# An attention and feed-forward kernel: stationary operands of 4, 32, 33 and 64 rows or columns widened to 128, and four small transposes made one

## The chip, the cores and the metric

The kernel runs on one core of a Trainium2 chip. The metric is the device time of one launch in microseconds; the kernel before takes 800.02 us (median of three runs, 799.88 to 800.47).

## What is computed

The input x has 8 batches of 512 tokens with 128 channels, float32. Three blocks follow each other, each with a residual:

```
x = x + 0.5 * ffn(layernorm(x))
x = x + attention(layernorm(x))
x = x + 0.5 * ffn(layernorm(x))
```

The feed-forward block has 512 hidden units, an exact GELU, and weights that depend on the batch: products of even and odd rows of tokens 1 to 16, scaled by 0.001, are added to both weight matrices.

```
even, odd = lt[:, ::2, :], lt[:, 1::2, :]          # lt: tokens 1 to 16 of x
m1 = (even[:, :4, :, None] * odd[:, :4, None, :]).reshape(B, 512, 128)
h = gelu(x @ W1.T + scale * x @ m1.T + b1)
out = h @ W2.T + scale * h @ m2.T + b2
```

The attention has 16 heads of 64. Queries and keys are RMS-normalised. The score of query i and key j gets a causal bias that depends on a learned gate of the key:

```
gate = softplus(einsum('bthd,hd->bht', k, u_n) / sqrt(64))
bias = -max(i - j, 0) * omega_eff[h] * gate[h, j]      # -inf where j > i
attn = softmax(q @ k.T / 8 + bias);  y = (attn @ v) @ Wproj
```

## The kernel before

Every engine runs one long, unrolled program. A table (ORDER) gives, by hand, the order of the stages on each engine: a lead, the first batch, a body used for the batches between, and a final part. A body holds stages of the batch itself, of the next one (its projections and first heads) and of the last one (its second feed-forward block). Engines wait for each other by semaphores.

**Precision.** Most products are made in 16-bit halves: `product` (L1048 to L1050) issues three matmuls, high by high, high by low and low by high. The low halves are computed by POOL and DVE.

**PSUM.** Banks 0 to 2 hold the scores, bank 3 the weighted values. Banks 4 to 7 are a ring: each stage that needs a bank takes the next (`part.room` waits until it has been evacuated, `filled_by` and `taken_by` signal). ACT and DVE evacuate it.

**Stages that the change touches**, by the names of the table:

- "m" on PE, `spread_even_tokens` (L1068 to L1077): for each feed-forward block, eight matmuls multiply a selection matrix `sel` (stationary, 64 rows x 128 columns) by the token rows `z_hl` (64 rows). 16 blocks in all, two a batch. Rows 0 to 31 of `z_hl` are high halves, rows 32 to 63 low halves.
- "out" on PE, `ffn_out` (L1096): the second product of the feed-forward block begins with a matmul that puts the bias into the bank; its stationary operand `ones` and its moving operand `b2rows` have 33 rows, of which 0 and 32 hold the bias.
- "gr" on PE, `gate_rows` (L1138 to L1144): the gates of eight heads, cut in high and low halves, stand as `gt[token, block, 4, 8]`. Four transposes, one for each block of 128 tokens, turn 32 columns each into 32 rows of 512. Twice a batch.
- "nm" on PE, `turn_max` (L1179): the row maxima of four heads stand in `maxima[token, block, head]`. Four transposes turn 4 columns each into 4 rows of 512. Four times a batch.

**What follows these transposes.** ACT copies the maxima rows, negated, to `nmt` (L1016, `take_max_rows`), DVE copies the gate rows to `gtt` (L1492, `take_gate_rows`). SP then issues, for each quad of heads, two DMAs from `gtt` (L729) and two from `nmt` (L748) into rows 64 to 67 and row 96 of `qk1`, so that the score matmuls add bias and maximum as further rows of the contraction. POOL makes the gates beforehand (`gates`, L849 to L854). The matmuls "a" of the max pass (L1170, 96 rows of `qk1`) wait for the gate rows, the scores "s" (L1197) for the maxima rows.

**Start.** DVE clears or fills a few tiles (L1279 to L1286) before its first layer norm.

Of the kernel before, what the change touches and what calls it, by code (L numbers as in the profile page):

```python
# [6 lines left out]
ALU = mybir.AluOpType  # L7
# [6 lines left out]
P = 128  # L14
# [281 lines left out]
def macaron(nc: bass.Bass, x, Wq, Wk, Wv, Wproj, q_rms_w, k_rms_w, omega, u, W1, b1, W2, b2, scale, out):  # L296
# [23 lines left out]
    with ExitStack() as ctx:  # L320
# [31 lines left out]
        b2cut = sb("b2cut", [LO_ROW + 1, C], F16)  # L352
        b2rows = sb("b2rows", [LO_ROW + 1, TB, C], F16)
        ones = sb("ones", [LO_ROW + 1, P], F16)
        sc = sb("sc", [P, 1])
# [34 lines left out]
        ROWS = 32  # L390
        z_hl = sb("z_hl", [2 * ROWS, C], F16)
        sel = sb("sel", [2 * ROWS, 2 * FB, P], F16)
        od = sb("od", [P, 2 * FB])
# [26 lines left out]
        softplus = sb("softplus", [P, TB, HH])  # L420
        gate = sb("gate", [P, TB, 2, HH])
        omr = sb("omr", [P, H])
        omj = sb("omj", [P, TB, 2, H])
        zero = sb("zero", [P, TB, 2, HH])
        gt = sb("gt", [P, TB, 4, HH], F16)
        gtt = sb("gtt", [4 * HH, T], F16)
        maxima = sb("maxima", [P, TB, H], F16)
        masked = sb("masked", [P, len(RING), T], F16)
        nmt = sb("nmt", [QH, T], F16)
        pt = sb("pt", [P, 2, SCOLS])  # L430
# [41 lines left out]
        def tokens(qd, t):  # L472
            return qkn[:, qd % 2, t // 2 * 2:t // 2 * 2 + 2, :, (t % 2) * P:(t % 2 + 1) * P]

        def of_heads(t):
# [199 lines left out]
        def _(sp):  # L675
# [42 lines left out]
            def place_operands(part, s, b, qd):  # L718

                if b == 0 and qd == 0:  # L720
                    sp.wait_ge(s_wv_lo, 1)
                    sp.wait_ge(s_wp_lo, 1)
                both = range(1) if b == 0 and qd < 2 else range(2)
                sp.wait_ge(s_hi, b * H + (qd + 1) * QH)
                for n in both:
                    place_upper(sp, qd, n)
                part.taken(sp, ("gr", qd // 2, s[-1]))
                for n in range(2):
                    sp.dma_start(qk1[GROW:GROW + 4, qd, n, 0, :, :],  # L729
                                 gtt[qd % 2 * 2 + n::4, :]).then_inc(s_gates[qd % 2], 16)  # L730
# [14 lines left out]
            def max_rows(part, s, b, qd):  # L745
                part.taken(sp, s)
                for n in range(2):
                    sp.dma_start(qk1[MROW:MROW + 1, qd, n, 1, :, :], nmt[n::2, :]).then_inc(s_mrow, 16)  # L748

# [10 lines left out]
        def _(pool):  # L760
# [23 lines left out]

            g.memset(zero[:, :, :, :], 0.0).then_inc(s_zero, 1)
            pool.wait_ge(s_zero, 1)
# [54 lines left out]
            def gates(part, s, b, hf):  # L841
                g2 = b * 2 + hf + 1
                if b == 0 and hf == 0:
# [4 lines left out]
                pool.wait_ge(s_softplus, g2)  # L848
                g.tensor_tensor(gate[:, :, :, :], softplus[:, :, :].unsqueeze(2).broadcast_to([P, TB, 2, HH]),  # L849
                                omj[:, :, :, hf * HH:(hf + 1) * HH], ALU.mult).then_inc(s_gate, 1)  # L850
                pool.wait_ge(s_gate, g2)
                g.tensor_tensor(gt[:, :, 0::2, :], gate[:, :, :, :], zero[:, :, :, :], ALU.add).then_inc(s_gt_h, 1)
                pool.wait_ge(s_gt_h, g2)
                g.tensor_tensor(gt[:, :, 1::2, :], gate[:, :, :, :], gt[:, :, 0::2, :], ALU.subtract).then_inc(s_gt, 1)  # L854

# [15 lines left out]
        def _(act):  # L871
# [138 lines left out]
            def take_max_rows(part, s, b, qd):  # L1010
# [3 lines left out]
                if g > 0:  # L1014
                    act.wait_ge(s_mrow, g * 32)
                part.taken_by(a.activation(nmt[:, :], part.bank(s)[0:QH, :].bitcast(F16)[:, 0:T], ACT.Copy, scale=-1.0), s)  # L1016

# [18 lines left out]
        def _(pe):  # L1036
# [101 lines left out]
            def gate_rows(part, s, b, hf):  # L1138
                pe.wait_ge(s_gt, b * 2 + hf + 1)
                part.room(pe, s)  # L1140
                for t in range(TB):
                    mm = pe.transpose(part.bank(s)[0:4 * HH, :].bitcast(F16)[:, t * P:(t + 1) * P],
                                      gt[:, t, :, :].rearrange("p r h -> p (r h)"), ident16[:, :])
                part.filled_by(mm, s)  # L1144

# [29 lines left out]
            def turn_max(part, s, b, qd):  # L1175
                part.taken(pe, ("a", qd * QH + QH - 1, s[-1]), 2, then=s)
                part.room(pe, s)
                for t in range(TB):
                    mm = pe.transpose(part.bank(s)[0:QH, :].bitcast(F16)[:, t * P:(t + 1) * P],  # L1179
                                      maxima[:, t, qd * QH:(qd + 1) * QH], ident16[:, :])  # L1180
                part.filled_by(mm, s)

# [86 lines left out]
        def _(dve):  # L1269
# [215 lines left out]
            def take_gate_rows(part, s, b, hf):  # L1485
# [15 lines left out]
            def row_maxima(part, s, b, h):  # L1501
                for i, blocks in enumerate(((3,), (2, 0), (1,))):
                    part.full(dve, s, i)
                    for ib in blocks:
                        col = 384 if len(blocks) == 2 and ib == 0 else 0
                        top = maxima[:, ib, h:h + 1]
                        if masked_by_dve(b, ib):
# [58 lines left out]
```

## Time and profile before

| | before |
|---|---|
| median of three runs | 800.02 us (799.88 to 800.47) |
| span of the profiled execution | 794.8 us |
| PE busy | 765.8 us (96%), 9669 matmuls |
| PE weight loads busy | 549.4 us (69%) |
| DVE busy | 667.6 us (84%), 1874 instructions |
| ACT busy | 655.8 us (83%), 1420 |
| POOL busy | 641.5 us (81%), 751 |
| one batch in the repeated part | 92.8 us |

For the profiled execution the page gives the span, from its first instruction to its last; the timed runs are device time of the whole launch, 5.2 us more than this span. A matmul's row shows the time from the first read to a modelled end, and matmuls overlap, so that the distance between two starts is shorter than the duration. The granted clock of PE is full after the first 55 us, in which it is at half for some stretches.

### The profile page before, as it was taken

How to read it: one execution, taken by the hardware profiler on the slowest of the kernel's cores; microseconds unless marked ns; L12 is line 12 of the kernel's file. 1: busy time of each engine (PE TensorE's matmuls, PEld its weight loads, DVE VectorE, ACT ScalarE, POOL GpSimd, SP SyncE). 2: the span in 40 equal slices, each digit the busy share in tenths (PEclk: the TensorE clock that was granted, in tenths of full speed). 3: DMA queues.
4: the chain of work that ended last, by engine and by line, in shares of the span. 5: the costliest groups of instructions: out<-in, count | busy, mean ns of one | idle time of the engine just before them, and what ended most of it. 6: DMA issues, size and time to landing. Idle time of an engine off the chain costs nothing.

```text
span 794.8 us, 25588 instructions
## 1 busy us (share of the span) xinstructions
PE 765.8 (96%) x9669; PEld 549.4 (69%) x9669; DVE 667.6 (84%) x1874; ACT 655.8 (83%) x1420; POOL 641.5 (81%) x751
## 2 busy tenths in 40 slices
PE   4789999999999999999999999999999999999997
PEld 2346767677767776677677777677776776777775
DVE  8779788987988887988989878888888889899965
ACT  6759877888998889897998889988897989986762
POOL 5528868978988979789888889889797897887791
PEclk9899999999999999999999999999999999999999
DMA  7071616464173633637153541736336371548420
GB/s 191 13 162 42 134 44 141 62 135 97 29 161 69 149 68 73 144 78 154 29 132 72 126 105 28 162 68 148 70 68 149 69 162 29 122 83 151 87 48 27
DMA packets 97297, 77.12 MB, mean 97 GB/s; under 512 B 71662, under 2 KB 84080, under 8 KB 97176
## 3 DMA queue, kind: packets, MB, share of 16 engines
q1 hardware_dynamic: 96696, 73.92, 43.6%
q10 hardware_dynamic: 480, 1.57, 0.8%
q8 instruction: 77, 1.26, 0.7%
q14 instruction: 44, 0.36, 0.1%
HBM read 4.74 MB, written 2.10 MB: 9 GB/s over the span
## 4 chain that ended last, share of the span: by engine, by line
PE 84%; ACT 4%; issue 3%; DVE 3%; DMA 2%; POOL 2%; SPq 1%; POOLq 0%; ACTq 0%; DVEq 0%
PE ps L1048 15%; PE ps L1049 14%; PE ps L1050 14%; PE ps L1197 8%; PE ps L1170 8%; PE ps L1198 8%; PE ps L1152 6%; PE ps L1199 3%; PE ps L1172 2%; DMA qk<-qkn 2%; PE ps L1065 1%; PE ps L1179 1%; ACT qkn L934 1%; PE ps L1075 1%; ACT sq L933 1%
## 5 line engine op out<-in xcount | busy, mean ns | idle before, releaser
L813 POOL TENSOR_TENSOR pt_l<-pt 128x512 f16<-128x512 f32 x368 | 320.3, 900 | 70.0 <-ACT pt L1008 69.8
L1008 ACT ACTIVATE pt<-ps 128x512 f32<-128x512 f32 (+1 forms) x384 | 175.1, 530 | 29.3 <-PE ps L1199 17.1
L839 POOL TENSOR_TENSOR qkn<-qkn,rs 128x512 f32<-128x512 f32 x128 | 130.5, 1048 | 30.9 <-ACT rs L945 30.9
L1197 PE MATMUL ps<-qk 128*128 128x512 f16 (+3 forms) x512 | 146.9, 300 | 0.0
L1198 PE MATMUL ps<-qk 128*128 128x512 f16 (+3 forms) x512 | 146.5, 299 | 0.0
L1508 DVE CUSTOM_DVE_ANT_0 masked<-ps,causal_row 128x512 f16<-128x512 f32 x224 | 130.4, 619 | 18.0 <-PE ps L1170 15.7
L1048 PE MATMUL ps<-v_buf,pt 128*128 128x65 f16 x1280 | 129.8, 194 | 0.9 <-POOL pt_l L813 0.8
L1049 PE MATMUL ps<-v_buf,pt 128*128 128x65 f16 x1280 | 129.8, 193 | 0.0
L1050 PE MATMUL ps<-v_buf,pt_l 128*128 128x65 f16 x1280 | 129.5, 193 | 0.0
L1048 PEld LDWEIGHTS ps<-v_buf,pt 128*128 128x128 bf16 x1280 | 118.0, 98 | 6.6 <-issue 1.2
L1049 PEld LDWEIGHTS ps<-v_buf,pt 128*128 128x128 bf16 x1280 | 117.5, 98 | 3.2
L1050 PEld LDWEIGHTS ps<-v_buf,pt_l 128*128 128x128 f16 x1280 | 117.6, 98 | 0.0
L933 ACT ACTIVATE sq<-ps 128x512 f32<-128x512 f32 x128 | 77.6, 606 | 37.1 <-PE ps L1050 33.2
L1170 PE MATMUL ps<-qk 96*128 96x512 f16 (+3 forms) x512 | 104.0, 300 | 3.7 <-DMA qk<-gtt 1.5
L1199 PE MATMUL ps<-causal_t,ident 128*128 128x128 f16 x512 | 105.6, 219 | 0.0
L1512 DVE TENSOR_REDUCE maxima<-ps 128x1 f16<-128x256 f32 (+3 forms) x288 | 95.9, 382 | 2.9 <-PE ps L1172 2.9
L1475 DVE TENSOR_REDUCE ss<-sq 128x8 f32<-128x512 f32 x128 | 83.8, 679 | 9.1 <-ACT sq L933 8.6
L817 POOL TENSOR_TENSOR ytt<-ytok,ytt 128x512 f16<-128x512 f32 x63 | 74.7, 1187 | 11.7 <-ACT ytt L1023 11.6
L934 ACT ACTIVATE qkn<-ps 128x512 f32<-128x512 f32 x128 | 78.2, 611 | 0.0
L1048 PE MATMUL ps<-wqkv_h,zt_h_att 128*128 128x512 f16 x192 | 74.0, 386 | 2.3 <-DVE zt_l_att L1408 1.0
L1049 PE MATMUL ps<-wqkv_l,zt_h_att 128*128 128x512 f16 x192 | 74.0, 385 | 0.0
L1050 PE MATMUL ps<-wqkv_h,zt_l_att 128*128 128x512 f16 x192 | 73.9, 385 | 0.0
(198 smaller groups left out, 2053.6 us busy)
## 6 DMA issues: line engine op xcount, KB each, us to landing
qk<-qkn SPq DMA_DIRECT2D x186, 256.0 KB, 4.1
x_in<-in_L_attn_x SPq DMA_DIRECT2D x8, 256.0 KB, 3.0
out<-x_out SPq DMA_DIRECT2D x8, 256.0 KB, 2.4
qk<-qkn ACTq DMA_DIRECT2D x6, 256.0 KB, 4.9
qk<-qk SPq DMA_DIRECT2D x1, 1024.0 KB, 8.5
qk<-gtt SPq DMA_DIRECT2D x64, 8.0 KB
qk<-nmt SPq DMA_DIRECT2D x64, 2.0 KB
y_hl<-ytt SPq DMA_TRANSPOSE x63, 3.1
```

Of the source, the lines that this page charges most:

```text
L813: g.tensor_tensor(pt_l[:, h % 2, c], pt[:, h % 2, c], pt_h[:, h % 2, c], ALU.subtract).then_inc(s_pt_l, 1)
L839: g.tensor_tensor(qk, qk, r.unsqueeze(4).broadcast_to([P, 2, 2, 2, D]), ALU.mult).then_inc(s_qkn, 1)
L1008: a.activation(pt[:, h % 2, c], ps[:, j, 0:width], ACT.Exp).then_inc(s_exp, 1)
L1048: pe.matmul(dst, ah, bh, start=first, stop=False)
L1049: pe.matmul(dst, ah, bl, start=False, stop=False)
L1050: return pe.matmul(dst, al, bh, start=False, stop=last)
L1170: mm = pe.matmul(dst, q1(h)[0:MROW, ib * P:keys], k1(h)[0:MROW, 0:keys], start=True, stop=by_dve)
L1197: pe.matmul(dst, k1(h)[:, keys], q1(h)[:, kb * P:T], start=True, stop=False)
L1198: pe.matmul(dst, k2(h)[:, keys], q2(h)[:, kb * P:T], start=False, stop=False)
L1199: mm = pe.matmul(dst[:, 0:P], ident16[:, :], causal_t16[:, :], start=False, stop=True)
L1508: ins = d.tensor_tensor_reduce(masked[:, part.unit(s, i)[0], col:col + (ib + 1) * P], part.bank(s, i)[:, col:col + (ib + 1) * P], causal_r ...
L1512: ins = d.tensor_reduce(top, part.bank(s, i)[:, col:col + (ib + 1) * P], AX.X, ALU.max)
```

## The change

`ones`, `b2rows`, `z_hl` and `sel` get 128 rows; the added rows are zero in `b2rows`, `z_hl` and `sel`. `maxima` becomes four tiles of 128 columns, one for each quad of heads, of which 16 (2 x 2 heads x 4 blocks) are written and the others stay zero; one transpose turns such a tile, and 16 rows of 128 columns hold what 4 rows of 512 held. The gates are laid out so that all 128 columns (4 x 4 x 2 x 4) are turned at once into 128 rows of 128. The copies of ACT and DVE and the DMAs of SP follow the new layout: the same bytes in pieces of 128 elements instead of 512. The order of the stages stays.

```diff
-        b2rows = sb("b2rows", [LO_ROW + 1, TB, C], F16)
-        ones = sb("ones", [LO_ROW + 1, P], F16)
+        b2rows = sb("b2rows", [P, TB, C], F16)
+        ones = sb("ones", [P, P], F16)
...
-        z_hl = sb("z_hl", [2 * ROWS, C], F16)
-        sel = sb("sel", [2 * ROWS, 2 * FB, P], F16)
+        z_hl = sb("z_hl", [P, C], F16)
+        sel = sb("sel", [P, 2 * FB, P], F16)
...
-        gate = sb("gate", [P, TB, 2, HH])
+        gate = sb("gate", [P, QH, 2, 2, TB])
...
-        gt = sb("gt", [P, TB, 4, HH], F16)
-        gtt = sb("gtt", [4 * HH, T], F16)
-        maxima = sb("maxima", [P, TB, H], F16)
+        gt = sb("gt", [P, QH, 4, 2, TB], F16)
+        gtt = sb("gtt", [P, P], F16)
+        maxima = sb("maxima", [P, H // QH, P], F16)
...
-        nmt = sb("nmt", [QH, T], F16)
+        nmt = sb("nmt", [QH * TB, P], F16)
...
+        def max_column(h, ib):
+            at = h % 2 * 2 * TB + h % QH // 2 * TB + ib
+            return maxima[:, h // QH, at:at + 1]
...
-                                 gtt[qd % 2 * 2 + n::4, :]).then_inc(s_gates[qd % 2], 16)
+                                 gtt[(qd % 2 * 2 + n) * 8 * TB:(qd % 2 * 2 + n + 1) * 8 * TB, :]).then_inc(s_gates[qd % 2], 16)
...
-                    sp.dma_start(qk1[MROW:MROW + 1, qd, n, 1, :, :], nmt[n::2, :]).then_inc(s_mrow, 16)
+                    sp.dma_start(qk1[MROW:MROW + 1, qd, n, 1, :, :].rearrange("o i (t c) -> o (i t) c", c=P), nmt[n * 2 * TB:(n + 1) * 2 * TB, :]).then_inc(s_mrow, 16)
...
-                g.tensor_tensor(gate[:, :, :, :], softplus[:, :, :].unsqueeze(2).broadcast_to([P, TB, 2, HH]),
-                                omj[:, :, :, hf * HH:(hf + 1) * HH], ALU.mult).then_inc(s_gate, 1)
+                g.tensor_tensor(gate[:, :, :, :, :].rearrange("p s r i t -> p t r i s"),
+                                softplus[:, :, :].rearrange("p t (i s) -> p t i s", s=QH).unsqueeze(2).broadcast_to([P, TB, 2, 2, QH]),
+                                omj[:, :, :, hf * HH:(hf + 1) * HH].rearrange("p t r (i s) -> p t r i s", s=QH),
+                                ALU.mult).then_inc(s_gate, 1)
...
-                part.taken_by(a.activation(nmt[:, :], part.bank(s)[0:QH, :].bitcast(F16)[:, 0:T], ACT.Copy, scale=-1.0), s)
+                part.taken_by(a.activation(nmt[:, :], part.bank(s)[0:QH * TB, :].bitcast(F16)[:, 0:P], ACT.Copy, scale=-1.0), s)
...
-                for t in range(TB):
-                    mm = pe.transpose(part.bank(s)[0:4 * HH, :].bitcast(F16)[:, t * P:(t + 1) * P],
-                                      gt[:, t, :, :].rearrange("p r h -> p (r h)"), ident16[:, :])
-                part.filled_by(mm, s)
+                part.filled_by(pe.transpose(part.bank(s).bitcast(F16)[:, 0:P],
+                                            gt[:, :, :, :, :].rearrange("p s r i t -> p (s r i t)"), ident16[:, :]), s)
...
-                for t in range(TB):
-                    mm = pe.transpose(part.bank(s)[0:QH, :].bitcast(F16)[:, t * P:(t + 1) * P],
-                                      maxima[:, t, qd * QH:(qd + 1) * QH], ident16[:, :])
-                part.filled_by(mm, s)
+                part.filled_by(pe.transpose(part.bank(s).bitcast(F16)[:, 0:P], maxima[:, qd, :], ident16[:, :]), s)
...
+            d.memset(maxima[:, :, :], 0.0)
+            d.memset(z_hl[2 * ROWS:P, :], 0.0)
+            d.memset(sel[2 * ROWS:P, :, :], 0.0)
...
-                part.taken_by(d.tensor_copy(gtt[:, :], part.bank(s)[0:4 * HH, :].bitcast(F16)[:, 0:T]), s)
+                part.taken_by(d.tensor_copy(gtt[:, :], part.bank(s).bitcast(F16)[:, 0:P]), s)
```

PE's program around a turn of the maxima rows in the body, with the projection of the next batch on both sides (`ps` is PSUM, the size is that of the output). Before:

```order
L1048 MATMUL ps<-wqkv_h,zt_h_att 128x512
L1049 MATMUL ps<-wqkv_l,zt_h_att 128x512
L1050 MATMUL ps<-wqkv_h,zt_l_att 128x512
L1179 MATMUL ps<-ident,maxima 4x128 x4
L1048 MATMUL ps<-wqkv_h,zt_h_att 128x512
L1049 MATMUL ps<-wqkv_l,zt_h_att 128x512
```

Changed:

```order
L1054 MATMUL ps<-wqkv_h,zt_h_att 128x512
L1055 MATMUL ps<-wqkv_l,zt_h_att 128x512
L1056 MATMUL ps<-wqkv_h,zt_l_att 128x512
L1182 MATMUL ps<-ident,maxima 128x128
L1054 MATMUL ps<-wqkv_h,zt_h_att 128x512
L1055 MATMUL ps<-wqkv_l,zt_h_att 128x512
```

Four transposes of 4 columns have become one of 128, in the same place.

DVE's program at the start, changed:

```order
L1284 MEMSET b2rows 128x256
L1285 MEMSET maxima 128x256
L1286 MEMSET z_hl 64x64
L1287 MEMSET sel 64x512
L1288 MEMSET y_hl 5x1024
L1290 CAST y_hl<-weff 2x1024
L1368 BN_STATS stats_a<-x_in 128x6 x4
```

The memsets of `maxima`, `z_hl` and `sel` are new; they stand ahead of the first statistics (sizes in 32-bit words where the tile is cleared).

## Rows read from the trace of the kernel before

**Rows 1.** The page: the chain that ended last, by engine.

```profile
PE 84%; ACT 4%; issue 3%; DVE 3%; DMA 2%; POOL 2%; SPq 1%; POOLq 0%; ACTq 0%; DVEq 0%
```

**Rows 2.** One batch's window: PE, PEld, DVE, ACT, POOL busy us; clock; DMA.

```profile
300.00:392.79 92.79, 92.65 (x1200) 67.43 (x1198) 79.60 (x230) 81.36 (x179) 80.97 (x93) 1.00 0.45 99
```

**Rows 3.** Waits in that window: total us, times, longest (PEld: weight loads).

```profile
POOL pt_l L813 <- ACT pt L1008: 8.0, 5, 2.9
...
PEld ps L1048 <- DVE qkn L1498: 1.1, 3, 0.5
```

**Rows 4.** Timeline of PE at a plain place: start, duration in us.

```profile
380.08 0.27 PE L1170 MATMUL ps<-qk 96*128 96x256 f16 x1
380.19 0.22 PE L1172 MATMUL ps<-causal_row,ident 128*128 128x128 f16 x1
380.25 0.38 PE L1197 MATMUL ps<-qk 128*128 128x512 f16 x1
```

**Rows 5.** Timeline of PE at a turn of the maxima rows.

```profile
303.28 0.38 PE L1049 MATMUL ps<-wqkv_l,zt_h_att 128*128 128x512 f16 x1
303.50 0.38 PE L1050 MATMUL ps<-wqkv_h,zt_l_att 128*128 128x512 f16 x1
303.81 0.39 PE L1179 MATMUL ps<-ident,maxima 128*4 128x128 f16 x4
304.13 0.39 PE L1048 MATMUL ps<-wqkv_h,zt_h_att 128*128 128x512 f16 x1
```

**Rows 6.** Timeline of PE at a turn of the gate rows.

```profile
310.90 0.60 PE L1152 MATMUL ps<-ident,qkn 128*128 128x128 f32 x4
311.43 0.40 PE L1142 MATMUL ps<-ident,gt 128*32 128x128 f16 x4
311.76 0.39 PE L1197 MATMUL ps<-qk 128*128 128x512 f16 x1
```

**Rows 7.** Timeline of PE at the bias row.

```profile
328.18 0.22 PE L1172 MATMUL ps<-causal_row,ident 128*128 128x128 f16 x1
328.33 0.39 PE L1096 MATMUL ps<-b2rows,ones 33*128 33x512 f16 x1
328.65 0.23 PE L1048 MATMUL ps<-w_h,hid 128*128 128x128 f16 x1
```

**Rows 8.** Timeline of PE at the spread of the tokens.

```profile
299.98 0.38 PE L1050 MATMUL ps<-wqkv_h,zt_l_att 128*128 128x512 f16 x1
300.29 0.62 PE L1075 MATMUL ps<-z_hl,sel 64*128 64x128 f16 x8
300.84 0.20 PE L1048 MATMUL ps<-v_buf,pt 128*128 128x65 f16 x1
```

**Rows 9.** Groups of PE and its weight loads: count, busy us, mean ns, idle before.

```profile
L1179 PEld LDWEIGHTS ps<-ident,maxima 128*4 128x4 f16 x128 | 6.4, 83 | 7.5 <-issue 6.0
L1048 PEld LDWEIGHTS ps<-wp_h,y_hl 128*128 128x128 f16 x256 | 25.0, 98 | 5.1 <-issue 2.5 <-DMA y_hl<-ytt 1.8
L1075 PE MATMUL ps<-z_hl,sel 64*128 64x128 f16 x128 | 10.3, 223 | 0.0
L1096 PE MATMUL ps<-b2rows,ones 33*128 33x512 f16 x16 | 6.2, 386 | 1.7 <-issue 1.7
```

**Rows 10.** Instructions on nmt and gate: duration ns min/median/max, first and last start.

```profile
L1016 ACT ACTIVATE nmt<-ps x32: 569/586/587, 59.2 to 754.1; 4x512 f16<-4x512 f16 x32
L849 POOL TENSOR_TENSOR gate<-softplus,omj x16: 319/322/323, 43.8 to 717.7; 128x64 f32<-128x64 f32 x16
```

**Rows 11.** The chain near 47 us; the SP timeline near 377 us.

```profile
46.67 2.42 DMA qk<-gtt
...
376.69 1.30 SPq L748 DMA_DIRECT2D qk<-nmt  x2
```

**Rows 12.** The DVE timeline at the start; the chain near 3 us.

```profile
1.68 0.27 DVE L1283 MEMSET b2rows<- 33x256 uint32 x1
...
2.80 2.96 DMA kw<-in_L_attn_k_rms_w
```

More of the change, by code:

```diff
@@ L420, in macaron @@
         softplus = sb("softplus", [P, TB, HH])
-        gate = sb("gate", [P, TB, 2, HH])
+        gate = sb("gate", [P, QH, 2, 2, TB])
         omr = sb("omr", [P, H])
         omj = sb("omj", [P, TB, 2, H])
-        zero = sb("zero", [P, TB, 2, HH])
-        gt = sb("gt", [P, TB, 4, HH], F16)
-        gtt = sb("gtt", [4 * HH, T], F16)
-        maxima = sb("maxima", [P, TB, H], F16)
+        zero = sb("zero", [P, QH, 2, 2, TB])
+        gt = sb("gt", [P, QH, 4, 2, TB], F16)
+        gtt = sb("gtt", [P, P], F16)
+        maxima = sb("maxima", [P, H // QH, P], F16)
         masked = sb("masked", [P, len(RING), T], F16)
-        nmt = sb("nmt", [QH, T], F16)
+        nmt = sb("nmt", [QH * TB, P], F16)
         pt = sb("pt", [P, 2, SCOLS])
@@ L783, in _ @@
                             pattern=[[1, P]], channel_multiplier=-1).then_inc(s_const, 1)
-            g.memset(zero[:, :, :, :], 0.0).then_inc(s_zero, 1)
+            g.memset(zero[:, :, :, :, :], 0.0).then_inc(s_zero, 1)
             pool.wait_ge(s_zero, 1)
@@ L848, in gates @@
                 pool.wait_ge(s_softplus, g2)
-                g.tensor_tensor(gate[:, :, :, :], softplus[:, :, :].unsqueeze(2).broadcast_to([P, TB, 2, HH]),
-                                omj[:, :, :, hf * HH:(hf + 1) * HH], ALU.mult).then_inc(s_gate, 1)
+                g.tensor_tensor(gate[:, :, :, :, :].rearrange("p s r i t -> p t r i s"),
+                                softplus[:, :, :].rearrange("p t (i s) -> p t i s", s=QH).unsqueeze(2).broadcast_to([P, TB, 2, 2, QH]),
+                                omj[:, :, :, hf * HH:(hf + 1) * HH].rearrange("p t r (i s) -> p t r i s", s=QH),
+                                ALU.mult).then_inc(s_gate, 1)
                 pool.wait_ge(s_gate, g2)
-                g.tensor_tensor(gt[:, :, 0::2, :], gate[:, :, :, :], zero[:, :, :, :], ALU.add).then_inc(s_gt_h, 1)
+                g.tensor_tensor(gt[:, :, 0::2, :, :], gate[:, :, :, :, :], zero[:, :, :, :, :], ALU.add).then_inc(s_gt_h, 1)
                 pool.wait_ge(s_gt_h, g2)
-                g.tensor_tensor(gt[:, :, 1::2, :], gate[:, :, :, :], gt[:, :, 0::2, :], ALU.subtract).then_inc(s_gt, 1)
+                g.tensor_tensor(gt[:, :, 1::2, :, :], gate[:, :, :, :, :], gt[:, :, 0::2, :, :], ALU.subtract).then_inc(s_gt, 1)
             def value_weights_lo(part, s, b):
@@ L1505, in row_maxima @@
                         col = 384 if len(blocks) == 2 and ib == 0 else 0
-                        top = maxima[:, ib, h:h + 1]
+                        top = max_column(h, ib)
                         if masked_by_dve(b, ib):
```

## The prediction

> **What bounds the kernel now.** I read the page's chain of waits first. It is 84% TensorE (PE); no other engine has more than 4% of it [rows 1]. Next the windows of one batch: in the middle of the run the same picture repeats every 92.8 us, and in the window 300.00 to 392.79 PE is busy for 92.65 us, ScalarE (ACT) for 81.36, GpSimd (POOL) for 80.97, VectorE (DVE) for 79.60, at the full granted clock [rows 2]. So in the repeated part PE's own order of work is the length of a batch, and each of the others has 11 to 13 us of idle time in it. The waits of that window say the same from the other side: the long ones are of POOL for ACT (8.0 us), while PE's weight loads wait for DVE by pieces of up to 0.5 us [rows 3]. A shorter PE is therefore a shorter kernel, until those small waits grow.
>
> The busy time hides how PE is spaced, because matmuls overlap and each row shows 0.2 to 0.4 us for a matmul that takes much less of PE. What counts is the distance from one start to the next. Two ordinary rows give the scale: a matmul of 256 columns starts at 380.08, the next at 380.19 and the one behind its 128 columns at 380.25 [rows 4], and a matmul of 512 columns takes from 303.28 to 303.50 [rows 5]. I work with 0.056 us for 128 columns and 0.216 us for 512, which print as 0.06 and 0.22. The first of these has 96 rows, and nothing is lost around it.
>
> **The change part by part.** I hold the four places that are edited against that scale.
>
> *Maxima rows.* The matmul ahead starts at 303.50 and has 512 columns, so the transposes could start at 303.72; they start at 303.81, 0.09 us late. Four of 0.056 us would let the next matmul start at 304.04; it starts at 304.13, 0.09 late again [rows 5]. So the stationary operand of 4 columns costs 0.18 us at its two edges. The change also drops three of the four transposes, 3 x 0.056 = 0.17 us. Together 0.35 us, 4 times a batch and 32 times in all: 11.3 us.
>
> *Gate rows.* Four float32 transposes start at 310.90 and take 0.11 us each, which would end at 311.34; the 32-column transposes start at 311.43, the matmul behind them at 311.76 instead of 311.65 [rows 6]. That is 0.20 us at the edges and 0.17 us for three transposes, 0.37 us, twice a batch and 16 times: 5.9 us.
>
> *Bias row* (33 rows). Start 328.33 where 328.24 was possible, next start 328.65, that is 0.32 us for 512 columns instead of 0.216 [rows 7]: 0.19 us, 16 times [rows 9]: 3.1 us.
>
> *Spread tokens* (64 rows). 0.09 us ahead (299.98 + 0.216 against 300.29), then 0.55 us for eight matmuls that need 0.45 [rows 8]: 0.19 us for each group of eight, 128 matmuls in all [rows 9], so 16 groups: 3.1 us.
>
> The four sum to 23.4 us, 2.9 us of each 92.8. The loss sits at both edges of all four kinds, at 4 and 32 columns as at 33 and 64 rows, with transposes and with plain matmuls, and it is absent at 96 rows. What they have in common is an operand that uses half of the array or less. I take it that full width removes it wholly. Four groups, one of each kind, lie at the very start or end where PE waits for something else anyway: minus 1.1 us, leaving 22.3.
>
> What the wider operand costs: its weight load takes 98 ns where 4 columns take 83 [rows 9], and loads run beside the matmul ahead of them; I cost it at nothing, at most 15 ns x 32 = 0.5 us if that cover were gone. The Trainium skill speaks against this edit here: "TensorE: Matmul & The Clock Gate", section "LDWEIGHTS (loading the stationary operand)", makes the load as long as its columns divided by 1.2 GHz, so 3 ns for 4 columns and 107 ns for 128. By that rule, uncovered, the maxima rows would give back 32 x 0.1 = 3.3 us; the rows above show 15 ns of difference, and I go by them.
>
> *ACT and DVE.* The copy of the negated maxima goes from 4 x 512 to 16 x 128 elements, the gate copy from 32 x 512 to 128 x 128. The first takes 0.58 us now [rows 10], and reads a quarter of the columns afterwards; if half of its time goes, 0.3 us, that is 4 times a batch. Neither engine bounds anything overall; locally it helps, since PE's ring of four banks waits for their evacuations. If a fifth of these 0.3 x 32 = 9.6 us reached PE it would be 2 us; I take 0 and keep 2 for the range.
>
> *POOL.* The gate product writes with a stride over the token blocks. It takes 0.32 us for 64 elements a row [rows 10]. Unchanged is one end; for the other I take three times the duration, 0.6 us more. POOL idles 12 us a batch [rows 2], so it matters only if the gate transposes come to wait; I take nothing, with 0.6 x 16 = 10 us as the far end.
>
> *DMA.* The bytes stay; the gate DMA goes from 8 pieces of 1 KB to 32 of 256 bytes, the maxima DMA from 2 of 1 KB to 8 of 256 bytes, 64 issues of each kind on SP. The gate DMA landed 2.42 us after its issue where it was waited for [rows 11]. For maxima the closest user is the score matmul at 380.25 [rows 4], and the pair of issues ends at 376.69 + 1.30 = 377.99 [rows 11], so 2.3 us are enough there today, and PE shows no wait. Longer by some tenths stays hidden; I take nothing.
>
> *Start.* DVE gets three more memsets ahead of the first statistics, 256 + 64 + 512 words where 256 words take 0.27 us [rows 12]: 0.9 us. The chain there runs through a DMA that lands at 5.76 [rows 12], with DVE's first layer norm just behind it, so part of it is hidden: between 0 and 0.9 us, I take 0.5.
>
> *What is late next.* The 2.9 us a batch come at ten places. After each PE reaches the next evacuation wait earlier; those by DVE already cost weight loads 1.1 us a batch at one line alone [rows 3]. Everything that other engines do for PE moves up too, as they wait for PE in turn and have 11 us to spare, so most passes. I charge 0.4 us a batch, 3.3 us.
>
> Sum: 22.3 - 3.3 - 0.5 = 18.5 us. The span is 794.8 us and the median of the three timed runs 800.02, so 5.2 us lie outside the span and stay. 800.0 - 18.5 = **781.5 us**.
>
> **The rivals.**
>
> *A. The other engines take back half.* The evacuations of the four-bank ring are what PE meets next; where the engine that evacuates is itself late with older work, the gain before that place is lost. For it: the load waits [rows 3]; against it: 11 to 13 idle us on each engine [rows 2]. Half of 22.3 gone and 0.5 at the start: 800.0 - 11.2 + 0.5 = 789.3.
>
> *B. The edges stay.* If the loss of 0.09 us comes from something else at these lines, only the dropped transposes count: 48 x 3 x 0.056 = 8.1 us, so 792.4. Against it: four kinds of work with the same edge, and none at 96 rows. The Trainium skill, "TensorEngine Tiling (Array Packing)", section "Key Properties", says that changing the tiling mode drains TensorE; that page puts operands of up to 64 rows or columns into the tiled modes, and the rows agree with 0.09 us at each edge.
>
> *C. Slower, by the small DMA pieces.* PE would wait where maxima and gate rows are first used. Take no slack at all for one use of the maxima rows and one of the gate rows a batch, the worst that rows allow. A landing later by d then costs 2d a batch, which passes the 2.9 saved when d is over 1.45 us: the landing of 2.42 us [rows 11] would have to grow by 60%. If it doubled, a batch would lose 4.84 - 2.9 = 1.9 us, 8 batches 15.5, and the kernel would take 815.5 us. The whole 2 KB or 8 KB is little beside the 256 KB copies on the same queue, which speaks against it. The Trainium skill, "DMA: Bandwidth & Descriptors", in the table at its head, wants 512 bytes for line rate and says that smaller transfers are read, modified and written; the same page says under "Why small descriptors are slow (HBM only)" that transfers within SBUF are spared the penalty. No row here shows a 256-byte piece by itself.
>
> **How the numbers follow.** The forecast has 0.72. A has 0.16, B 0.05, C 0.04, and 0.03 is left for losses at the DMAs or on POOL that happen to cancel the gain. This kernel's runs spread by 0.6 us, so 0.2%, 1.6 us, is about what a measurement can tell from no change. The low end takes everything through plus 2 us from ACT and nothing at the start: 800.0 - 22.3 - 2 = 775.7, so 776. The high end takes in A: 789.5. Between them lie the forecast's case and most of A, 8 in 10. Faster by over 0.2%: 0.72 + 0.16 + 0.05 = 0.93; within it 0.03; slower 0.04.
>
> **What would show it.** The starts around each edited line should stand 0.056 us (128 columns) and 0.216 us (512) apart, with no loss at the edges; one transpose of 128 x 128 for four. A batch should last about 90.4 us. PE's waits for DVE and ACT should grow by tenths, ACT's copy of the maxima should fall to about 0.3 us. If the edges still show 0.09 us, B is right. If matmuls of the scores wait for the DMA from nmt or gtt, C is. If the batch is near 91.5 us with clean edges, A is, and the waits of PE's loads will name the engine.

## The result and the profile after

The change makes the kernel slower: 817.38 us (median of four runs, 811.30 to 819.81) against 799.95 (798.04 to 800.47) beside it, a ratio of 1.022 with the interval 1.018 to 1.026, clear of 1. Forecast was 781.5, and slower had a chance of 4 in 100.

| | before | after |
|---|---|---|
| median | 799.95 us | 817.38 us |
| span of the profiled execution | 794.8 us | 816.6 us |
| mean granted clock of PE | 0.994 | 0.979 |
| PE busy | 765.8 us | 763.4 us |
| DVE busy | 667.6 us | 681.7 us |
| POOL busy | 641.5 us | 639.5 us |

Lines after the edited places are 3 to 6 higher in this program. First the chain that ended last, by engine, of the kernel after:

```profile
PE 61%; POOL 12%; DVE 10%; ACT 7%; issue 4%; DMA 3%; SPq 1%; POOLq 0%; ACTq 0%; DVEq 0%
```

PE had 84% of it [rows 1]. Now two batches of after, one behind the other, in the windows view (length, then busy us of PE, its weight loads, DVE, ACT, POOL; clock; DMA share and GB/s):

```profile
283.26:381.22 97.96, 92.88 (x1184) 68.04 (x1182) 82.53 (x230) 80.08 (x179) 81.12 (x93) 0.98 0.44 94
381.22:473.00 91.78, 90.77 (x1184) 66.84 (x1181) 78.17 (x230) 79.81 (x179) 80.87 (x93) 1.00 0.48 100
```

The same work takes 97.96 us in one and 91.78 in the other, where the kernel before needs 92.79 [rows 2]. DVE is busy 4.4 us longer in the slow one. One instruction does that. Here is the line of DVE that makes the layer norm's shift, in the trace of after, and the same in that of before (count: shortest, median and longest duration in ns):

```profile
L1385 DVE SCALAR_TENSOR_TENSOR shift_c<-mv_c,rstd_c x7: 154/4912/4921, 185.5 to 763.0; 128x4 f32<-128x4 f32 x7
```

```profile
L1381 DVE SCALAR_TENSOR_TENSOR shift_c<-mv_c,rstd_c x7: 149/726/728, 187.0 to 740.9; 128x4 f32<-128x4 f32 x7
```

Four elements a row, and 4.9 us in five batches of after. The timelines of DVE, POOL and ACT at one of them (start, duration; in brackets the idle time before and what ended it):

```profile
283.34 4.91 DVE L1385 SCALAR_TENSOR_TENSOR shift_c<-mv_c,rstd_c 128x4 f32<-128x4 f32 x1
```

```profile
281.06 2.04 POOL L836 TENSOR_TENSOR hid_l<-hid 128x512 f16<-128x512 f32 x2
283.05 5.18 POOL L817 TENSOR_TENSOR pt_l<-pt 128x512 f16<-128x512 f32 x6
```

```profile
288.29 0.49 ACT L965 ACTIVATE z_a<-x,shift_c,rstd_c 128x128 f32<-128x128 f32 x1 [4.98 <-DVE shift_c L1385]
```

shift_c starts while POOL is in the first of six back-to-back subtractions (`pt_l`, heads 5 and 6), and ends with the last of them: 283.34 + 4.91 = 288.25, POOL 283.05 + 5.18 = 288.23. In the kernel before it meets the same series and ends with the *first* subtraction:

```profile
279.79 0.72 DVE L1381 SCALAR_TENSOR_TENSOR shift_c<-mv_c,rstd_c 128x4 f32<-128x4 f32 x1
```

```profile
279.45 5.18 POOL L813 TENSOR_TENSOR pt_l<-pt 128x512 f16<-128x512 f32 x6
```

So DVE and POOL exclude each other here, and DVE is let in either at the end of one POOL instruction or only when the whole run of them is over. In all 78 cases of the thirteen kernels in which this meeting is left to itself (listed below), it ends 16 to 24 ns after the end of a POOL subtraction. The Trainium skill, "SBUF — State Buffer", section "SBUF: two separate sides", says that a VectorE operation with two SBUF inputs and a GpSimd one that reads SBUF share a port pair, which the first to start keeps for its whole instruction while the other fully blocks. The 0.72 us agree with that rule; 4.9 us over six instructions are more than it tells.

PE has work queued behind it. This is PE's wait in the 9 us of after from 283.3 on (total us, times, longest), and a piece of its timeline:

```profile
PE ps L1071 <- ACT z_a L965: 3.0, 2, 2.6
```

```profile
288.92 0.30 PE L1071 MATMUL ps<-ident,z_a 128*128 128x128 f32 x1 [2.59 <-ACT z_a L965]
...
290.54 0.19 PE L1054 MATMUL ps<-v_buf,pt 128*128 128x65 f16 x1
290.57 0.20 PE L1055 MATMUL ps<-v_buf,pt 128*128 128x65 f16 x1
...
291.28 0.24 PE L1055 MATMUL ps<-v_buf,pt 128*128 128x65 f16 x1
291.33 0.25 PE L1056 MATMUL ps<-v_buf,pt_l 128*128 128x65 f16 x1
```

PE stands still for 3 us. Its granted clock, full until then, falls to the lower of its two levels (1.2 instead of 2.4 GHz) from 291.1 us for 3.4 us; matmuls of 65 columns start every 0.03 us ahead of that and every 0.05 to 0.06 behind it.

What the prediction was about has happened as told. Turns of the maxima, the spread of the tokens, a turn of the gates and the bias row in after, in the batch that was not held:

```profile
384.02 0.22 PE L1056 MATMUL ps<-w_h,hid_l 128*128 128x128 f16 x1
384.07 0.22 PE L1182 MATMUL ps<-ident,maxima 128*128 128x128 f16 x1
384.13 0.61 PE L1071 MATMUL ps<-ident,z_a 128*128 128x128 f32 x4
...
401.12 0.38 PE L1056 MATMUL ps<-wqkv_h,zt_l_att 128*128 128x512 f16 x1
401.33 0.61 PE L1081 MATMUL ps<-z_hl,sel 128*128 128x128 f16 x8
401.78 0.19 PE L1054 MATMUL ps<-v_buf,pt 128*128 128x65 f16 x1
...
412.37 0.22 PE L1147 MATMUL ps<-ident,gt 128*128 128x128 f16 x1
412.43 0.38 PE L1198 MATMUL ps<-qk 128*128 128x512 f16 x1
...
429.13 0.38 PE L1102 MATMUL ps<-b2rows,ones 128*128 128x512 f16 x1
429.35 0.22 PE L1054 MATMUL ps<-w_h,hid 128*128 128x128 f16 x1
```

0.05 or 0.06 us for 128 columns, 0.45 for the eight of the spread, and 0.21 or 0.22 for 512, no 0.09 at an edge [rows 5 to 8]. So there are two questions: what holds shift_c, and why even the batch without a hold saves 1.0 us instead of 2.4.

### The profile page after: what moved, and what is told of

Read it like the earlier page. It is cut to its first block, busy times and chain, and to the rows that moved or that the text cites. A ratio compares the mean times of both kernels' runs of the same rounds, so it can differ in the third digit from the quotient of the medians.

```text
span 816.6 us, 25303 instructions
## 1 busy us (share of the span) xinstructions
PE 763.4 (93%) x9525; PEld 551.7 (68%) x9525; DVE 681.7 (83%) x1877; ACT 644.5 (79%) x1420; POOL 639.5 (78%) x751
## 4 chain that ended last, share of the span: by engine, by line
PE 61%; POOL 12%; DVE 10%; ACT 7%; issue 4%; DMA 3%; SPq 1%; POOLq 0%; ACTq 0%; DVEq 0%
PE ps L1054 10%; PE ps L1056 10%; PE ps L1055 10%; PE ps L1174 6%; PE ps L1198 6%; PE ps L1199 6%; PE ps L1156 6%; POOL pt_l L817 5%; POOL qkn L843 5%; DVE shift_c L1385 3%; PE ps L1200 3%; DMA qk<-qkn 2%; PE ps L1071 2%; DVE masked L1512 1%; DVE maxima L1516 1%
## 5 line engine op out<-in xcount | busy, mean ns | idle before, releaser
L1198 PE MATMUL ps<-qk 128*128 128x512 f16 (+3 forms) x512 | 149.5, 305 | 0.0
L1199 PE MATMUL ps<-qk 128*128 128x512 f16 (+3 forms) x512 | 149.3, 304 | 0.0
L1054 PE MATMUL ps<-v_buf,pt 128*128 128x65 f16 x1280 | 133.8, 196 | 3.2 <-issue 2.0
L1055 PE MATMUL ps<-v_buf,pt 128*128 128x65 f16 x1280 | 133.8, 196 | 0.0
L1056 PE MATMUL ps<-v_buf,pt_l 128*128 128x65 f16 x1280 | 133.5, 195 | 0.0
L1054 PEld LDWEIGHTS ps<-v_buf,pt 128*128 128x128 bf16 x1280 | 120.5, 99 | 9.4 <-issue 4.6
L1055 PEld LDWEIGHTS ps<-v_buf,pt 128*128 128x128 bf16 x1280 | 119.9, 99 | 3.4
L1056 PEld LDWEIGHTS ps<-v_buf,pt_l 128*128 128x128 f16 x1280 | 119.9, 99 | 0.0
```

The lines of the kernel that those rows point to most:

```text
L1054: pe.matmul(dst, ah, bh, start=first, stop=False)
L1055: pe.matmul(dst, ah, bl, start=False, stop=False)
L1056: return pe.matmul(dst, al, bh, start=False, stop=last)
L1198: pe.matmul(dst, k1(h)[:, keys], q1(h)[:, kb * P:T], start=True, stop=False)
L1199: pe.matmul(dst, k2(h)[:, keys], q2(h)[:, kb * P:T], start=False, stop=False)
```

## The experiments

Times are medians, beside the kernel before on the same chip. All kernels but e2, e5 to e12 and e18 start from the changed one.

**Take the instruction apart.** e1 makes shift_c in four instructions of one column each; e2 does the same in the kernel before.

```diff
-d.scalar_tensor_tensor(shift[n][:, :], mv[n][:, :, 0], -1.0, rstd[n][:, :], ALU.mult, ALU.mult)
+for t in range(TB):
+    d.tensor_scalar(shift[n][:, t:t + 1], mv[n][:, t, 0:1], rstd[n][:, t:t + 1], -1.0, ALU.mult, ALU.mult)
```

> The changed kernel, with the one DVE instruction that makes the layer-norm shift (L1385, reads two SBUF operands, 128x4, 4.91 us in five of six batches against 0.73 before) replaced by four TENSOR_SCALAR of 128x1 that read one SBUF operand each. Theory P (this instruction is held while POOL works): no instruction at that line over 0.5 us, z_a no longer waits 5 us, no half clock after 60 us, 780 to 790 us. Rival D (small DMA pieces): nothing changes, 811 to 820. Rival C (the clock falls because PE's work is thinner): stretches at half clock stay, over 805.

> The kernel before with the same replacement. Theory P: there the instruction was held for 0.73 us a batch for the second feed-forward block and for up to 0.98 in the first, with little of it on PE's path: 795 to 800 us. The distance from this kernel to e1_shift_split is then the change's own worth, 12 to 20 us. Rivals D and C: this one stays at 800 and the distance is negative, as for the change.

e1: 794.68 us (ratio 0.9954, 0.9939 to 0.997), no piece over 0.22 us, repeated batches of 92.2 to 93.4 us, and full clock from 60 to 780 us. The hold went as expected, but the time lies above the 780 to 790 us that I gave. e2: 801.68 (1.0043, 1.0026 to 1.0061). Form e1's row:

```profile
L1386 DVE TENSOR_SCALAR shift_c<-mv_c,rstd_c x28: 202/204/215, 187.0 to 740.2; 128x1 f32<-128x1 f32 x28
```

The changed kernel is 22.7 us faster with this one instruction replaced, and no longer slower than the kernel before: the hold accounts for the whole of the slowdown. From e2 to e1, both without a hold, the change is worth 7.0 us, where I expected 12 to 20.

**Take the meeting away.** e3 lets POOL wait for shift_c ahead of the series; e7 does it in the kernel before.

```diff
 n = b * H + h
+if h == 5 and 1 <= b <= B - 2:
+    pool.wait_ge(s_shift["c"], b)
```

> The changed kernel, the two-operand instruction kept, but POOL waits for the shift's semaphore before the two heads of subtractions (head 5) that ran beside it. Theory P: the instruction takes 0.15 us, POOL starts those about 0.5 us later, 780 to 790 us, within 3 us of e1_shift_split. Rivals D and C: 811 to 820, since neither DMA pieces nor PE's density are touched.

e3: **791.77 us** (790.24 to 793.45), ratio 0.9924 (0.9899 to 0.9949): the fastest of all, faster than both kernels, if just outside the 780 to 790 us expected. shift_c takes 0.16 us, and POOL's wait costs it half a us:

```profile
276.86 0.16 DVE L1387 SCALAR_TENSOR_TENSOR shift_c<-mv_c,rstd_c 128x4 f32<-128x4 f32 x1
```

```profile
277.10 5.18 POOL L819 TENSOR_TENSOR pt_l<-pt 128x512 f16<-128x512 f32 x6 [0.46 <-DVE shift_c L1387]
```

From 817.38 to 791.77 are 25.6 us for five held batches, 5.1 each: 4.75 us of DVE, most of which would reach PE, and what the low clock adds; the split between the two was not measured.

**What decides whether it is held?** I first looked at where shift_c starts in the running subtraction: in after and before, 271 to 288 ns after its start in the held cases, 332 to 335 in those let in. e4 puts a memset ahead of shift_c on DVE; e5 and e6 put one and two memsets (128x1) ahead of head 5 on POOL, in the kernel before; e11 puts one of 128x36 there, sized for the middle of that band.

```diff
+if h == 5 and 1 <= b <= B - 2:
+    g.memset(nudge[:, :], 0.0)
```

> The changed kernel with one memset of 128x1 on DVE ahead of the shift of the second feed-forward block, which moves it about 0.06 us later against POOL's run. Before, it began 0.33 us after the start of a POOL instruction and was let in at its end; changed, it began 0.27 to 0.29 us after and was held for six of them. Theory P with the phase deciding: the start moves to 0.33 to 0.37 us after, 0.7 us long, 780 to 790 us. Theory P without the phase (held whenever POOL is busy enough): 4.9 us stay, 811 to 820.

> The kernel before with one memset of 128x1 on POOL ahead of the six subtractions of head 5 (batches 1 to 6), which moves POOL's series by some 35 to 60 ns against DVE's shift_c. In the kernel before shift_c starts 333 ns after the subtraction that runs, and is let in at its end. Theory (the hold depends only on when shift_c starts within a running subtraction; held cases lay at 269 to 288 ns, the nearest let in at 332): it now starts near 270 to 300 ns; where it is at or below 288 it is held over the series, 4.9 us, and the kernel before becomes slower by up to 20 us (near 815 to 820) without any part of the change; at 295 to 330 it tells where the border lies. Rival (the hold comes from the changed tiles or layouts): shift_c stays at 0.73 us and the time within 1 us of 799.2.

> The same with two such memsets, 70 to 120 ns. Theory of the phase: shift_c starts 210 to 265 ns into the subtraction. If held cases form a band around 270 to 290, it may be let in at the first end (0.75 to 0.85 us) and the time stays within 1.5 us of 799.2; if it lands within 265 to 290, it is held, 4.9 us in most batches, near 815 to 820. Rival (changed tiles or layouts): 0.73 to 0.85 us in all batches, no band.

> The kernel before with one memset of 128x36 on POOL ahead of the six subtractions of head 5 (batches 1 to 6). One memset of one column moved shift_c's start from 333 to 304-316 ns after the start of the running subtraction, two moved it to 261-268, and it was let in at the first end in both. The 36 columns are chosen to bring it to 273-286 ns. Theory (there is a narrow band, seen at 269 to 288 ns, in which shift_c is held over the whole series of six): 4.9 us instead of 0.73 in most of batches 1 to 6, half the clock for some us after each, and a kernel some 15 to 20 us slower, near 812 to 819, with nothing of the change in it. Rival (the hold belongs to something in the changed program, such as the new layouts or the places of tiles): 0.78 us in each batch and a time within 1.5 us of the kernel before.

e4: 813.63 (1.0191, 1.0176 to 1.0207), let in twice at 347 and 348 ns, held four times at 269 to 282. e5: 799.34 (1.0009, 0.9995 to 1.0023), at 304 to 316 ns, let in. e6: 798.75 (1.0004, 0.9987 to 1.002), at 261 to 268, let in. e11: 798.18 (0.9989, 0.9974 to 1.0004), at 263 to 276 ns in all six batches, let in six times. My theory of a band fell with e11.

The second theory was that the overlap of the two POOL instructions counts (the next starts some 42 ns ahead of the end of the last), which the memset of e11 had parted. e12 moves the memset one instruction back in the kernel before, so that the last `hid_l` and the first `pt_l` stand as in the held cases, with nothing between; e13 puts 128x1 between them in the changed kernel; e14 puts it in the middle of the six.

> The kernel before with one memset of 128x28 on POOL ahead of the last subtraction of hid_l, one instruction earlier than in e11, so that the last hid_l and the first pt_l follow each other directly. In every held case so far the last hid_l ended 231 to 246 ns ahead of shift_c's start and the first pt_l started 269 to 288 ns ahead of it; in the kernel before these are 290 and 333, and this memset moves both by about 53. Theory a (the hold is decided in the overlap of those two subtractions): held in most of batches 1 to 6, shift_c 4.9 us, the kernel 12 to 20 us slower than before, 811 to 819. Theory b (it belongs to the changed program): shift_c 0.78 us, time within 1.5 us of before.

> The changed kernel with one memset of 128x1 on POOL between the last subtraction of hid_l and the first of head 5 (batches 1 to 6): 42 ns more or less on POOL, nothing else. Theory a: no two subtractions overlap at the critical moment, shift_c is let in at the first end, 0.78 us, and the kernel takes 791 to 795, as with the wait in e3. Theory b, or if the end of hid_l alone decides: still 4.9 us and near 817.

> The changed kernel with one memset of 128x1 on POOL between the subtractions of head 5 and those of head 6, that is in the middle of the series of six. If a held shift_c is let in as soon as an instruction stands there that does not use the port: 2.4 us instead of 4.9 in the held batches (three subtractions of 1.0, 1.0 and 0.6 us less the phase of 0.27), and a time near 800. If the hold lasts until POOL stands still: 4.95 us and near 818.

e12: 799.08 (1.001, 0.9998 to 1.0022). DVE and POOL there:

```profile
278.84 0.78 DVE L1384 SCALAR_TENSOR_TENSOR shift_c<-mv_c,rstd_c 128x4 f32<-128x4 f32 x1
```

```profile
277.49 0.13 POOL L834 MEMSET nudge<- 128x28 f32 x1
277.56 1.04 POOL L835 TENSOR_TENSOR hid_l<-hid 128x512 f16<-128x512 f32 x1
278.56 2.62 POOL L814 TENSOR_TENSOR pt_l<-pt 128x512 f16<-128x512 f32 x3
```

278.84 is 0.28 us into the subtraction, the place of the held cases to within 10 ns, on both sides of the boundary, and it is let in six times of six. e13: 816.17 (1.024, 1.0201 to 1.0279), held four times, at 236 to 244 ns, and let in twice at 300 and 303, though no two subtractions overlap at the start of the series. Both theories of the moment itself are wrong. e14 varied from run to run, 799.72 to 816.45 us over nine runs with the median 811.99. In the profiled one, of 804.77 us, its memset let shift_c in twice, after 2.35 us, and three times it did not (4.95 us), so neither expectation holds as it stands; how many batches were held in the other runs is not known:

```profile
277.70 2.35 DVE L1388 SCALAR_TENSOR_TENSOR shift_c<-mv_c,rstd_c 128x4 f32<-128x4 f32 x1
```

```profile
277.43 2.61 POOL L820 TENSOR_TENSOR pt_l<-pt 128x512 f16<-128x512 f32 x3
279.98 0.10 POOL L811 MEMSET nudge<- 128x1 f32 x1
280.03 2.61 POOL L820 TENSOR_TENSOR pt_l<-pt 128x512 f16<-128x512 f32 x3
```

**Which part of the change?** Three kernels take one part back each, with no wait.

> The change without its gates part (rows and maxima only), no wait added. If the hold hangs on any gain of time on PE that brings shift_c nearer to the series: held where the first pt_l starts less than 295 ns ahead, 4.9 us, 795 + 4.5 us for each batch that is held. If it hangs on the gates part (their 256-byte DMAs land in this stretch): shift_c 0.73 to 0.8 us in all batches, and about 793 us.

> The change without its maxima part (rows and gates only). If the hold hangs on the maxima part (DVE writes the maxima to other columns just ahead of shift_c): 0.73 to 0.8 us in all batches and about 794 us, at whatever alignment. If not: held where the first pt_l starts less than 295 ns ahead, and 4.5 us more for each.

> The change without its widened rows (maxima and gates only). The rows touch nothing on the other engines, so if the hold hangs on timing alone it may go either way here, by where the first pt_l starts (held below 295 ns); let in at all batches: about 797 us, near the kernel before; held in five of six: about 818 us.

e15: 823.52 (1.032, 1.0284 to 1.0355), held in six of six batches at 217 to 223 ns. e16: 814.46 (1.022, 1.0177 to 1.0264), held in five at 285 to 291, let in once at 336. e17: 796.38 (0.9961, 0.9945 to 0.9978), let in six times at 342 to 347. So the widened rows seemed to be needed. But looking further back along POOL, the held cases had one more thing in common. In them POOL works without a pause for over 10 us ahead of shift_c. Some 9 us ahead, the second of its two `w_l` subtractions meets a DVE instruction, `ytok`. In all cases let in, it starts 61 to 67 ns after ytok; in all held ones, 115 to 178 ns after it. In 39 of the cases let in, and in none held, POOL also pauses between the two `w_l` (0.03 to 0.65 us). Five cases of e5 were let in without such a pause, so the pause is not needed. e5, e6, e11 and e12 moved POOL only after that. e18 moves it ahead of `w_l`, in the kernel before, with nothing of the change:

```diff
 part.taken(pool, s, 0)
+if n == "a" and b >= 2:
+    g.memset(nudge[:, :], 0.0)          # 128 x 142, 0.21 us
 g.tensor_tensor(w_l[:, 0, :], weff[:, 0, :], w1_h, ALU.subtract)
```

> The kernel before with one memset of 128x142 on POOL ahead of the first w_l subtraction (batches 2 to 7), sized to move w_l by 153 ns to where it stands in the held cases: the second w_l 9.06 us ahead of shift_c instead of 9.13, the series 60 ns later from there on, the first pt_l 270 to 290 ns ahead of it. If only the alignment of the whole series counts: held, 4.9 us in most of batches 1 to 6, 811 to 819 us. If the widened rows are needed: let in, 0.78 us, and within 1.5 us of the kernel before.

e18: **822.08 us** (820.51 to 824.40), ratio 1.0299 (1.0271 to 1.0328). POOL's timeline of e18, then that of before at the same place; then `ytok` and shift_c on DVE in e18, and `ytok` in before:

```profile
271.34 0.21 POOL L824 MEMSET nudge<- 128x142 f32 x1
271.52 1.03 POOL L825 TENSOR_TENSOR w_l<-weff 128x512 f16<-128x512 f32 x1
272.51 1.15 POOL L828 TENSOR_TENSOR w_l<-weff,w_h 128x512 f16<-128x512 f32 x1
...
277.32 4.02 POOL L835 TENSOR_TENSOR hid_l<-hid 128x512 f16<-128x512 f32 x4
281.31 5.16 POOL L814 TENSOR_TENSOR pt_l<-pt 128x512 f16<-128x512 f32 x6
```

```profile
269.57 1.03 POOL L822 TENSOR_TENSOR w_l<-weff 128x512 f16<-128x512 f32 x1
270.66 1.16 POOL L825 TENSOR_TENSOR w_l<-weff,w_h 128x512 f16<-128x512 f32 x1
```

```profile
272.39 0.42 DVE L1526 TENSOR_TENSOR ytok<-ps,rden 128x256 f32<-128x256 f32 x1
...
281.58 4.92 DVE L1384 SCALAR_TENSOR_TENSOR shift_c<-mv_c,rstd_c 128x4 f32<-128x4 f32 x1
```

```profile
270.60 0.42 DVE L1523 TENSOR_TENSOR ytok<-ps,rden 128x256 f32<-128x256 f32 x1
```

The second `w_l` stands 0.12 us behind ytok in e18 (272.51 against 272.39), 0.06 before (270.66 against 270.60), and shift_c is held in five of six batches. In the sixth `w_l` stood 63 ns behind ytok. A memset of 0.21 us in each of six batches costs 24 us, a little more than expected. These are the thirteen kernels that leave the meeting to itself, six batches of each profiled execution (ns: from the start of the running `pt_l` to shift_c, and from ytok to the second `w_l`):

| | held | `pt_l` to shift_c | ytok to `w_l` | let in | `pt_l` to shift_c | ytok to `w_l` |
|---|---|---|---|---|---|---|
| before | 0 | | | 6 | 332-335 | 63-65 |
| after | 5 | 271-288 | 121-129 | 1 | 332 | 64 |
| e4 | 4 | 269-282 | 129-136 | 2 | 347-348 | 63-66 |
| e5 | 0 | | | 6 | 304-316 | 65-67 |
| e6 | 0 | | | 6 | 261-268 | 63-64 |
| e11 | 0 | | | 6 | 263-276 | 61-63 |
| e12 | 0 | | | 6 | 279-283 | 62-64 |
| e13 | 4 | 236-244 | 122-128 | 2 | 300-303 | 61-62 |
| e14 | 5 | 269-292 | 115-129 | 1 | 341 | 61 |
| e15 | 6 | 217-223 | 174-178 | 0 | | |
| e16 | 5 | 285-291 | 118-124 | 1 | 336 | 65 |
| e17 | 0 | | | 6 | 342-347 | 63-65 |
| e18 | 5 | 267-277 | 124-127 | 1 | 336 | 63 |

Held are all 34 cases in which `w_l` starts 115 ns or more behind ytok (two of them, in e14, only up to the memset), let in all 44 in which it is 61 to 67. The position at the moment itself does not separate the two: 261 to 283 ns was let in 18 times, in e6, e11 and e12. With e18 this shows that no part of the change is needed. The hold goes with how POOL's series stands to DVE's from some 9 us back, and the change moved that. It does not show that the meeting of `w_l` and ytok decides. POOL and DVE run on from there in the same order, so every later meeting moved with it. e5, e6, e11 and e12 show only that POOL can be moved from the last `hid_l` on without a hold. Which meeting decides, and by what mechanism, stays open. In e3 `w_l` stands 130 to 137 ns behind ytok in four of six batches, the place of the held cases, and its wait keeps shift_c at 0.16 us there too.

**How much does each part give, without the hold?** e7 to e10 have e3's wait, e7 with nothing else, the others with one part of the change.

> The kernel before with POOL's wait for shift_c ahead of head 5's subtractions, as in e3: the base for the three parts that follow. In the kernel before shift_c takes 0.73 us, not 4.9, so the wait has little to give: theory 797 to 799.5, the kernel before 798 to 799 on the same chip.

> e7 and of the change only the widened rows (z_hl, sel, ones, b2rows with 128 rows): nothing changes on any other engine, and the prediction's price is 6.2 us less on PE. Full pass: 5.5 to 6.2 us below e7. Rival A (other engines take back three quarters, as e3 suggests for the whole): 1.5 to 2 us below e7.

> e7 and of the change only the maxima turned by one transpose (with ACT's shorter copy and eight-piece DMAs): priced at 11.3 us on PE. Full pass: 10 to 11 us below e7. Rival A: 3 to 5 below. Small DMA pieces (rival C of the prediction): no gain, score matmuls wait for the DMA to nmt's row.

> e7 and of the change only the gates turned by one transpose: priced at 5.9 us on PE. Full pass: 5 to 5.9 us below e7. Rival A: 1.5 to 2 below. The three parts together were 22 us on PE and e3 had about 7 of them; if the three single gains sum to much more than 7, the loss comes from what they share (another engine's chain that becomes the bound); if they sum to 7, each part meets its own wait.

| | priced on PE | measured, ratio to before |
|---|---|---|
| e7, wait alone | | 799.08, 1.0005 (0.999 to 1.002) |
| e8, rows | 6.2 us | 794.48, 0.9943 (0.9929 to 0.9957) |
| e9, maxima | 11.3 us | 798.32, 0.9989 (0.9977 to 1.0002) |
| e10, gates | 5.9 us | 798.21, 0.9993 (0.9979 to 1.0006) |
| e3, all three | 23.4 us | 791.77, 0.9924 (0.9899 to 0.9949) |

The wait alone changes nothing that can be measured, as expected. The rows pass three quarters of their price, 4.6 of 6.2 us, less than the 5.5 that I gave at least. The largest item, the maxima, passes 0.9 of 11.3, the gates 0.6 of 5.9, and both intervals take in no gain at all. Full pass and rival A both had more; rival C had no gain for e9, but in its trace from 60 to 760 us PE's weight loads wait for a DMA from `nmt` once, for 0.3 us, so it is not C. The three gains sum to 6.0 us beside 6.1 for e3 by its ratio (0.76% of 799), each with an interval of about 1 us to either side. So they add up as far as can be told, which speaks for separate waits and does not prove them. One can be read at the end of a batch. POOL, PE and ACT there in the kernel before:

```profile
337.96 4.04 POOL L839 TENSOR_TENSOR qkn<-qkn,rs 128x512 f32<-128x512 f32 x4 [1.31 <-ACT rs L945]
341.96 2.61 POOL L813 TENSOR_TENSOR pt_l<-pt 128x512 f16<-128x512 f32 x3
```

```profile
334.00 0.38 PE L1050 MATMUL ps<-wqkv_h,zt_l_att 128*128 128x512 f16 x1
...
344.68 0.19 PE L1048 MATMUL ps<-v_buf,pt 128*128 128x65 f16 x1
```

```profile
334.41 0.60 ACT L933 ACTIVATE sq<-ps 128x512 f32<-128x512 f32 x1 [1.00 <-PE ps L1050]
...
337.67 0.22 ACT L945 ACTIVATE rs<-ssl 128x16 f32<-128x16 f32 x1
```

And in e3:

```profile
518.47 4.05 POOL L845 TENSOR_TENSOR qkn<-qkn,rs 128x512 f32<-128x512 f32 x4 [1.10 <-ACT rs L953]
522.48 2.61 POOL L819 TENSOR_TENSOR pt_l<-pt 128x512 f16<-128x512 f32 x3
```

```profile
514.50 0.38 PE L1058 MATMUL ps<-wqkv_h,zt_l_att 128*128 128x512 f16 x1
...
525.19 0.19 PE L1056 MATMUL ps<-v_buf,pt 128*128 128x65 f16 x1 [0.41 <-issue]
```

The third projection from the end of the batch on PE releases ACT, which then works without a pause up to `rs` (334.41 to 337.89 before, 514.91 to 518.39 in e3). That releases POOL's four products `qkn`, and behind them on POOL stand the three subtractions `pt_l` of head 15, which PE's next weighted values need. From the last matmul of that projection to their end are 10.57 us before (344.57 - 334.00) and 10.59 in e3 (525.09 - 514.50). PE takes 10.68 us from one to the other before, and 10.69 in e3. PE starts 0.1 us behind POOL's end in both: there was no slack before. Two turns of the maxima lie between, priced at 0.7 us, and all that they save is waited away. A batch of e3 lasts 91.8 us, where full pass would be 89.9, so this place has about a third of the loss; the rest was not traced to its places.

## Why the prediction was wrong

**What bounds the kernel.** The step "each of the others has 11 to 13 us of idle time in it" was true as a sum and wrong as slack. POOL's idle time lies where it waits for ACT [rows 3]; at the end of a batch its chain runs from there back to PE with nothing to spare. I read the waits of PE in that batch, which showed nothing for POOL because they were just at nought.

**The four places.** Right: the edges went to nothing, at all four kinds and to 10 ns wherever the next matmul did not wait for another engine, and rival B is dead. The start cost about 0.5 us as said: POOL's first memset of `qk` moved from 7.60 to 8.08 us, PE's first spread of the tokens from 9.7 to 10.1.

**"What is late next".** Mis-sized. I charged 3.3 us of the 22.3. e3 is 6.1 us faster than before by its ratio, 7.4 by the medians, so 14 to 16 us were taken back (22.3 - 0.5 less that), about two thirds. A batch without a hold lasts 91.8 us, where I had 90.4 for a clean one and 91.5 for rival A. Rival A is what the change does apart from the hold, and it is even a little harder than I drew it; its price of 789.3 is near e3's 791.8, its chance of 0.16 was far too low. Its mechanism fits in part: what PE waits for at the place shown is no evacuation of the ring but the subtractions at the end of a chain through ACT and POOL.

**The other engines.** ACT's copy fell from 586 to 249 ns, as taken. POOL's products stayed at 0.32 us. The DMAs in small pieces caused no wait that counts: PE's longest for the gate rows, at the start, went from 1.5 to 1.7 us, and the unheld batch shows none for a DMA. Rival C gave a time near the measured one, 815.5, by a mechanism that did not occur.

**The step that turned the sign** is missing: I priced what each instruction costs and what it waits for, and not what it meets. The row was there, shift_c with 726 ns for four elements, five times what it takes alone (149), beside POOL's series; it says that DVE waits for POOL at this place in each batch. Yet not every shift does it: 0.02 to 0.07 us just ahead of the series left it at 0.7 to 0.8 us (e5, e6, e11, e12), and 0.06 us of the whole series from `w_l` on made 4.9 of it (e18), on the path of PE. So the row gave reason for a rival with a price, not for a forecast of slower; I had no such rival.

**Two readings of times.** The 5.2 us were not all outside the span: in every run of the record with both figures the device time is 2.0 us above its span. By that the profiled execution of the kernel before took about 796.8 us (an estimate), less than the three timed ones. The sum does not hang on it. And the spread of 0.6 us came from three runs; in the experiments the kernel before took 796.4 to 801.7 us, so a difference of a few tenths of a per cent needs many runs.

## What to carry to other kernels

Look in the trace before for small instructions that take several times their own shortest duration beside another engine's series. Here such a row (726 ns against 149) marked a place where two engines exclude each other, and a change of timing, a faster one at that, turned it into a stall of 4.9 us. One wait that orders the two took the hold away (e3) and cost the kernel before nothing that could be measured (e7). Idle time of an engine is slack only if the chain that runs through it from PE and back has some: measure from the instruction that releases it to the one that waits, and compare with what PE takes in between. And time a change also with such a meeting taken away, or its gain can't be seen under it.

## What was new of the hardware

An exclusion between DVE and POOL can outlast the instruction that causes it: 4.9 us over six back-to-back subtractions of 0.6 to 1.04 us, with five ends at which DVE was not let in. The position at the moment itself does not decide it. At the start of the program something like it shows with memsets on POOL, `om_e` on DVE (16 elements a row) and four memsets of 0.95 us. In the kernel before, then in e8:

```profile
8.52 0.94 DVE L1291 TENSOR_SCALAR om_e<-om 128x16 f32<-128x16 f32 x1
```

```profile
8.84 2.73 DVE L1295 TENSOR_SCALAR om_e<-om 128x16 f32<-128x16 f32 x1
```

It took 2.73 us in e8, e10, e11, e16 and e18 and 0.94 or 0.95 in the others. The second memset started 31 to 36 ns ahead of it in the first and 26 to 38 in the others, so its place tells nothing here either. What differed was not found, and no run took POOL's memsets away.
